# Edge aggregation of a two-layer graph attention network: sums of destination groups in two PSUM banks, and gather indices copied by GpSimd

## The reference

```python
def gat_layer(x, W, a_src, a_dst, bias, src, dst, heads, out_c, concat):
    h = (x @ W).reshape(n, heads, out_c)
    ...
    ex = jnp.exp(e - m[dst])
    z = jax.ops.segment_sum(ex, dst, num_segments=n)
    alpha = ex / (z[dst] + 1e-16)
    msg = h[src] * alpha[:, :, None]
    out = jax.ops.segment_sum(msg, dst, num_segments=n)
```

## Time and profile before

| | |
|---|---|
| median of 3 runs | 3121.55 us (3118.72 to 3125.71) |
| the profiled execution | 3143.92 us, its span 3142.2 us |
| mean granted TensorE clock | 0.729 |
| busy share of the span | PE 58%, PEld 39%, DVE 43%, ACT 26%, POOL 48% |
| mean DMA rate | 185 GB/s |

### The profile page before, as it was taken

How to read it: one execution, slowest core, us unless ns; L and a number is a source line. 1 busy time by engine, 2 the same in 40 slices (tenths; PEclk the granted TensorE clock), 3 DMA queues, 4 the chain that set the end, 5 groups by cost and what they waited for, 6 DMA issues and landing times. The chain is left out here.

```text
span 3142.2 us, 49939 instructions
## 1 busy us (share of the span) xinstructions
PE 1827.9 (58%) x14982; PEld 1225.0 (39%) x14983; DVE 1341.1 (43%) x2284; ACT 811.8 (26%) x2185; POOL 1513.4 (48%) x1379
## 2 busy tenths in 40 slices
PE   4578884045565556364666845555555473299980
PEld 3444553033343333232333423333333373277760
DVE  7656558465565556593773010000000383011116
ACT  3211110123333333342112323333233320033330
POOL 0356665176677767443222565555555333321216
PEclk9788896566666666687897955666666555699995
DMA  4311110177887878523553778888888691244549
GB/s 145 83 37 49 28 33 18 62 243 248 257 255 246 255 244 257 182 66 109 196 181 133 242 246 272 268 270 271 274 269 274 219 314 68 57 159 157 170 145 396
DMA packets 182780, 580.88 MB, mean 185 GB/s; under 512 B 49267, under 2 KB 51314, under 8 KB 182472
## 3 DMA queue, kind: packets, MB, share of 16 engines
q0 software_dynamic: 81744, 351.62, 35.6%
q1 hardware_dynamic: 75790, 159.71, 15.3%
q10 hardware_dynamic: 25200, 69.03, 5.7%
HBM read 473.74 MB, written 106.49 MB: 185 GB/s over the span
## 5 line engine op out<-in xcount | busy, mean ns | idle before, releaser
L1257 POOL DMA_INDIRECT ring<-feat_tab,islot x392 | 429.0, 1094 | 241.9 <-issue 102.1
L1341 PE MATMUL acc<-ring,work 128*32 128x192 f32 x3904 | 351.5, 481 | 304.0 <-ACT work L1403 180.1
L1296 DVE TENSOR_TENSOR work<-iota_f,dst_rel 128x224 f32<-128x224 f32 x112 | 43.9, 392 | 670.1 <-PE acc L1341 373.5
L641 POOL DMA_INDIRECT work<-score_tab,islot x224 | 236.0, 1054 | 153.0 <-DVE islot L694 84.8
L1341 PEld LDWEIGHTS acc<-ring,work 128*32 128x32 f32 x3904 | 146.4, 140 | 384.0 <-issue 340.8
L1257 POOL DMA_INDIRECT work<-feat_tab,islot x224 | 240.6, 1074 | 111.8 <-issue 56.1
L1407 ACT ACTIVATE work<-work 32x192 f32<-32x192 f32 x800 | 287.7, 360 | 10.7
L1341 PE MATMUL acc<-work 128*32 128x192 f32 (+1 forms) x2208 | 199.1, 453 | 133.5 <-ACT work L1403 79.5
L1341 PE MATMUL acc<-big,work 128*32 128x192 f32 x1744 | 161.7, 474 | 152.7 <-ACT work L1403 101.3
L1050 PE MATMUL acc<-wg,work 128*128 128x384 f32 x600 | 226.2, 528 | 19.7 <-ACT work L1107 19.7
L598 PE MATMUL acc<-wg,work 128*128 128x384 f32 x600 | 220.8, 521 | 18.6 <-issue 15.3
(11 more groups left out here) (354 smaller groups left out, 3367.6 us busy)
## 6 DMA issues: line engine op xcount, KB each, us to landing
slot_out<-ring SPq DMA_DIRECT2D x57, 384.0 KB, 2.3
agg_raw<-work ACTq DMA_DIRECT2D x50, 388.0 KB
ring<-agg_raw SPq DMA_DIRECT2D x50, 388.0 KB
feat_tab<-work ACTq DMA_DIRECT2D x50, 384.0 KB
ring<-lo_rows SPq DMA_DIRECT2D x49, 256.0 KB, 6.8
ring<-in_x SPq DMA_DIRECT2D x25, 384.0 KB
work<-in_x SPq DMA_DIRECT2D x25, 384.0 KB
mid_rows<-work ACTq DMA_DIRECT2D x25, 384.0 KB, 2.8
```

The costliest lines, as they stand in the source:

```text
L641: pool.indirect_dma_start(sg[:, h, k * H:(k + 1) * H], None, score_tab[0], bass.IndirectOffsetOnAxis(ap=islot[:, h * 8 + k:h * 8 + k + 1], ...
L1257: pool.indirect_dma_start(rows[k][:, 0:C], None, feat_tab[l], bass.IndirectOffsetOnAxis(ap=islot[:, h * UN + k:h * UN + k + 1], axis=0)).t ...
L1296: ins = V.tensor_tensor(out, near.to_broadcast([P, BATCH, WIN]), dst_rel[:, cols].unsqueeze(2).to_broadcast([P, BATCH, WIN]), ALU.is_equal)
L1341: m = nc.tensor.matmul(sums_ps[c * WIN:(c + 1) * WIN, 0:n], hot, row[:, c * CHUNK:c * CHUNK + n], start=start, stop=True, skip_group_check ...
```

## The change

- The sums of groups alternate between PSUM banks `acc[:, 0]` and `acc[:, 1]` (`BANKS = 2`). The semaphore `flushed` starts one ahead, so a group waits only until the sums of the group two before it have been taken. A register of TensorE holds the bank of the open group, and since a matmul's bank is fixed in the instruction, each tile and each opening has two copies of its matmuls, chosen by `If`/`Else`.
- The close writes its element into `tps` instead of `acc[:, 1]`.
- ScalarE copies the quarters directly from PSUM; the copy into `stage` and `stage` itself are gone. `flushed` is now told by the copy of the weight sums. There are two `onehot_x`, and `next_hot` is made three groups ahead instead of two.
- The indices are copied by GpSimd, seven at a time, right ahead of the seven gathers that use them, and GpSimd waits for its own copy. VectorE's copy of 14 is gone.

```diff
-        onehot_x = agg_part(WIN)
-        stage = [agg_part(CHUNK + ZC) for _ in range(2)]
-        zeros = stage[1]
+        onehot_x = [agg_part(WIN) for _ in range(2)]
+        zeros = agg_part(CHUNK + ZC)
...
+                    def indices(i, h, j):
+                        cols = slice(h * UN + j * BATCH, h * UN + (j + 1) * BATCH)
+                        nc.gpsimd.tensor_copy(islot[:, cols], src_t[:, ds(i * UN + j * BATCH, BATCH)]).then_inc(idx_ready, 1)
+                        pool.wait_ge(idx_ready, i * 2 + (j + 1))
+
+                    def turn(i, h, done):
+                        for j in range(2):
+                            indices(i, h, j)
+                            pool.sem_inc(tick_p, 1)
+                            for k in range(j * BATCH, (j + 1) * BATCH):
+                                pool.wait_ge(tile_mm, done + min(k + 2, UN) if isinstance(done, int) else done + (k + 2))
+                                pool.sem_inc(tick_p, 1)
+                                gather(k, h)
...
+                    def place(bank, c, a, z):
+                        return acc[c * WIN:(c + 1) * WIN, bank, a:z]
+
+                    def added(i, k, t, j):
+                        if k % BATCH == 0:
+                            pe.wait_ge(hot_ready, i * 2 + (k // BATCH + 1))
+                        if l == 0:
+                            pe.wait_ge(msg_ready, t + 1)
+                        else:
+                            pe.wait_ge(row_in[k], i * 16 + 16)
+                        sums(onehot[:, k, :], k, t, False, j).then_inc(tile_mm, 1)
+
+                    def opened(b, k, t, j):
+                        pe.wait_ge(open_ready, b)
+                        pe.wait_ge(flushed, b)
+                        sums(onehot_x[j], k, t, True, j).then_inc(open_mm, 1)
...
-                        nc.tensor.matmul(acc[0:WIN, 1, 0:1], iota_f[:, 0:WIN], iota_f[:, 0:1], start=True, stop=True,
+                        nc.tensor.matmul(tps[0:WIN, 0, 0:1], iota_f[:, 0:WIN], iota_f[:, 0:1], start=True, stop=True,
...
-                            sums(onehot[:, k, :], k, t, False).then_inc(tile_mm, 1)
+                            bank = pe.snap(bank_reg, min_val=0, max_val=BANKS - 1)
+                            with pe.If(bank > 0):
+                                added(i, k, t, 1)
+                            with pe.Else():
+                                added(i, k, t, 0)
                             with pe.If((bits & (1 << k)) > 0):
...
                                 with pe.Fori(b0 + 1, b1 + 1) as b:
-                                    pe.wait_ge(open_ready, b)
-                                    pe.wait_ge(flushed, b)
-                                    sums(onehot_x, k, t, True).then_inc(open_mm, 1)
+                                    pe.reg_mov(bank_reg, b & (BANKS - 1))
+                                    bank = pe.snap(bank_reg, min_val=0, max_val=BANKS - 1)
+                                    with pe.If(bank > 0):
+                                        opened(b, k, t, 1)
+                                    with pe.Else():
+                                        opened(b, k, t, 0)
...
+                    act.sem_inc(flushed, BANKS - 1)
+
...
-                            nc.scalar.activation(stage[w % 2], sums_ps, ACT.Copy).then_inc(flushed, 1)
-                            next_hot(q + 2)
-                            act.wait_ge(flushed, q + 1)
                             for c in range(4):
                                 nc.scalar.activation(raw[sl][w * WIN:(w + 1) * WIN, c * CHUNK:(c + 1) * CHUNK],
-                                                     stage[w % 2][c * WIN:(c + 1) * WIN, 0:CHUNK], ACT.Copy)
-                            m = nc.scalar.activation(raw[sl][w * WIN:(w + 1) * WIN, C:ROW],
-                                                     stage[w % 2][zp:zp + WIN, CHUNK:CHUNK + ZC], ACT.Copy)
-                            m.then_inc(blk_ready, 1)
-                        act.wait_ge(blk_ready, b * WPB + WPB)
+                                                     acc[c * WIN:(c + 1) * WIN, w % BANKS, 0:CHUNK], ACT.Copy)
+                            nc.scalar.activation(raw[sl][w * WIN:(w + 1) * WIN, C:ROW],
+                                                 acc[zp:zp + WIN, w % BANKS, CHUNK:CHUNK + ZC], ACT.Copy).then_inc(flushed, 1)
+                            next_hot(q + 3, (w + 3) % 2)
+                        act.wait_ge(flushed, b * WPB + (WPB + BANKS - 1))
```

More of the change, by code:

```diff
@@ L1319, in turn @@
                             hots(i, j)
-                            if j == 1 and not last:
-                                indices(i + 1, 1 - h)
                             if l == 0:
                                 messages(i, j)
-                    turn(0, 0, first=True)
+                    turn(0, first=True)
                     with dve.Fori(0, TURNS // 2 - 1) as i:
@@ L1354, in _ @@
                     for c in range(4):
[L1355 removed]
+                        m = nc.tensor.matmul(acc[c * WIN:(c + 1) * WIN, 0, 0:CHUNK + ZC], zeros[:, 0:WIN], zeros, start=True, stop=True,
                                              skip_group_check=True)
```

59 lines of the change are left out of this document (22 added, 37 removed).

## The result

The changed kernel takes 3183.1 us (median of 4 runs, 3174.1 to 3190.9) against 3123.6 us (3118.7 to 3130.2) for the kernel before on the same chip: a ratio of 1.0162, 95% interval 1.0123 to 1.0201. It is slower by some 60 us, where 28 us less were forecast.

The account below looks back on a forecast made before the run. GpSimd was taken to nearly fill layer 0 and TensorE to set layer 1. Layer 0 +12 us and layer 1 -40 us gave -28 us, from 3121.6 to 3094 us; range 3015 to 3172 us, the forecast's own 3070 to 3112.

Parts of the forecast that it names:

- What bounds the kernel: Aggregation stages: GpSimd 90% occupied in layer 0, 62 us real waiting; TensorE sets layer 1, waiting 241.0 us for evictions.
- Two banks: Hand-offs between groups: eviction wait disappears, TensorE's sequencer (about 0.9 us) is next; layer 1 gains 45 us, layer 0 next to nothing.
- mere delay: Rival, late matmul results: they idle TensorE without being work; layer 1 -80, layer 0 -20, 3022 us; chance 0.17.
- the late results: Closing matmuls in layer 1: results come 2.69 us after the recorded end in the example; taken as work, not delay.
- The choice of a bank: TensorE's sequencer, every tile and opening: 0.35 us a tile, 137 us a layer plus 35 for openings, hidden where the unit lags.
- The indices on GpSimd: Index copies ahead of gathers: 56 a layer at 0.94 us, 53 us a layer added to GpSimd's floor.
- Evictions straight from PSUM: ScalarE's evictions: copy L1403 (0.337 us, 100 a layer) goes, bank freed later but before its need; gains nothing.
- The sum: Both stages: layer 0 +12 us (bounds -20, +53), layer 1 -40 us (bounds -96, +20), together -28 us.
- the four signs named for being wrong: Profile after: copies under 0.3 us in all; layer 1 under 580 us; layer 0 gaining like layer 1; instruction packets by the hundred.
- GpSimd is the bound: Rival, GpSimd's gathers: copies come on top, layer 0 +50 us, layer 1 -5, about 3166 us; chance 0.33.
- TensorE's loop no longer stays loaded: Rival, TensorE's instruction fetch: doubled body refetched, six packets a turn, some 170 us, 3290 us; chance 0.04.

Follow-up runs that it names:

- e11_banks2: Changed kernel's two banks and bank choice by test per tile, but indices copied by VectorE as before; 1.0140 to the kernel before (third set).
- the control: Kernel before plus register operations per close that bound the two group numbers, which all follow-up kernels have; 1.0029 to the kernel before.
- e14_pool2: Kernel before with only GpSimd's index copies, seven at a time directly ahead of the gathers, one bank; 1.0091 to the kernel before (fourth set).
- c_before: Code name of the control: kernel before plus register operations per close; 1.0029 to the kernel before (second set).
- e8_free: Ideal second bank without choice: all tiles summed in bank 0, ScalarE copies out unwritten bank 1, output wrong, indices by VectorE; 0.9885 to the kernel before.
- e13_pairs_banks: Two banks, indices by VectorE, group end and bank tested for two tiles at once where no group ends; 1.3230 to the kernel before.
- e2_pool: Kernel before with only GpSimd's index copies directly ahead of the gathers, one bank; 1.0417 to the kernel before (first set, faster chip).
- e1_banks: Changed kernel without GpSimd's copies, indices by VectorE as before; 1.0834 to the kernel before (first set, faster chip).

## Why the prediction was wrong

**What bounds the kernel.** Right that no engine is full and that GpSimd alone nearly fills layer 0. Missed: "This stage is set by TensorE", said of layer 1 by default, was read from waits and never applied to the sequencer of TensorE, for which no busy share stands in the page.

**Two banks.** Right in mechanism and nearly in size. The wait is gone, the sequencer is next (1.16 us from close to load after, 0.9 forecast), and the value of the ideal bank was 45 us in layer 1 and about nothing in layer 0; measured 35 us in all, on another chip, with 13 to 19 us in layer 0. The decision against mere delay held; that the late results are ordinary work did not quite, since loads go in at 0.70 us each there.

**The choice of a bank: the step that failed.** The price per tile was right: 0.35 us was taken, and the quickest tiles of layer 0 stand 0.98 us apart in the changed kernel (0.97 in e11_banks2) and 0.62 in the kernel before. The time in branches rose by 222 us over both stages. What was wrong is the sentence "It is hidden where the matrix unit lags behind its sequencer", which entered the sum as zero for layer 0 and as a bound of +20 us for layer 1. Alone the choice costs 160 us (152 over the control), and 82 us beside the second bank, where 0 and at most +20 had been entered. Late results are poor cover: they appear at closes, at the end of a group's burst of tiles, and when the tiles come more slowly the queue never fills, the evictions are less late (2.94 to 2.01 us from close to load in layer 1), and the time has moved from one place to the other. The comparison that should have been made is the tile's distance, 0.75 us in the earlier trace rows, against its matmuls: where a burst runs at the sequencer's pace, each test lengthens the burst. The prediction wrote just that ("would be felt wherever it isn't hidden") and then counted it nowhere in layer 0. Nor is it felt in full: of the 344 us that the prediction reckoned for both layers, 152 show alone, 82 beside the bank, and 253 on the faster chip. No run gives a way to forecast that share.

**The indices on GpSimd.** 0.94 us per copy was forecast. Measured: the intervals before gathers 0 and 7 grew by 1.1 to 1.3 us in layer 0 and 0.4 to 0.9 in layer 1, and the others became shorter. With one bank they cost 19 us over the control, in the change itself 0.2% at most (1.0162 against 1.0140 on another chip, 1.0844 against 1.0834 on one). The copy's wait does what was said; its place in the sum, +12 us for layer 0, was near for a kernel without the choice (layer 0 of e14_pool2 is 19 us longer than that of c_before, layer 1 as long).

**Evictions straight from PSUM.** As said: ScalarE is busy 51 us less per layer (the earlier trace rows and the windows above), and nothing follows from it.

**The sum.** Layer 0 was to grow by 12 us and grew by 36; layer 1 was to shrink by 40 and shrank by 5. By the runs: -35 for the bank and +82 for the choice beside it (e11_banks2 less e8_free), which together are only e11_banks2's +47 again, and some 7 for the copies, within the noise between two sets: +54 us, where +60 were measured. The stated range ended at 3172 us, though the bounds of the two layers, +53 and +20, add up to 3195; the 644 us of TensorE time in layer 1 stand in no row (the stage takes 658). Layer 0 was to stay within 20 us of 659 and took 696, layer 1 was to be near 618 and took 653. But of the four signs named for being wrong none came: the list held nothing for a TensorE that is slower tile by tile.

**The rivals.** "GpSimd is the bound" gave 3166 us, near the 3183 measured, and only by luck: without its copies the kernel is as slow. "Mere delay" is refuted by e8_free. "TensorE's loop no longer stays loaded" was rightly held unlikely (23 packets), but its price, 170 us, was nearly six times too small (e13_pairs_banks stands 960 us above e11_banks2). Its six packets a turn and 0.5 us each came from no row; measured are ten packets a turn and 3.1 us for a branch that waits for them, with nothing of it covered. No rival said that the choice simply costs more than the bank brings; its terms (172 us of sequencer time a layer) stood in the prediction, and as a rival with half of it uncovered it would have given 3121.6 + 172 - 45 = 3249 us; a range that reached toward it would have held the result.

## What to carry to other kernels

A decision in a loop costs its branches on the engine's own sequencer, 0.2 us for each that jumps. Wherever the loop's short distances (here tile to tile) are the sequencer's, that time belongs in the sum, with nothing and the full price as bounds; here a quarter to three quarters of it were felt. "The unit lags behind" is no reason to put it at nothing: when the burst slows down, the lag shrinks with it. Before removing a wait, price an ideal version that leaves part of the work out (here 1.15%), and compare it with what the removal has to add. Copies that feed a gather did best several gathers ahead of it. Doubling a loop's arms is to be counted in instructions against what stays loaded.

## What was not expected of the hardware

The same kernel takes 2833 us on one chip and 3122 to 3128 us on the others. With GpSimd's copies (e2_pool and e14_pool2, the same kernel) the eviction starts 0.09 us after a close in layer 1 on the first and 1.61 us on the other (medians), at the same granted clock of 0.67, and that stage takes 559 and 650 us. Which resource differs wasn't found. The same change (e1_banks and e11_banks2) costs 8.3% on the one and 1.4% on another.

A program whose loop of TensorE no longer stays loaded lost 18 us in each turn of 14 tiles, making the two stages 1.76 times as long, though all that it moved was 9.3 MB.
